# Score operands of 128 rows instead of 97, and the mixing of the experts as four pieces in separate steps

## The reference, cut to what matters

```python
sx = einsum('bsh,ndh->bnsd', x, hl_w) + hl_b          # 4 heads of 16 features
q  = einsum('bnsd,neod->bneso', sx, wq)               # 4 experts per head
k, v = ...                                            # one per head
scores = einsum('bnesd,bntd->bnest', q, k) * d**0.5 + causal
att = softmax(scores);  out = att @ v                 # per head and expert
gs  = softmax(out @ gate_w + gate_b)                  # weights of the experts
mixed = einsum('bnsed,bnse->bnsd', out, gs)           # the mixing of the experts
hn = layernorm(mixed + resid)
hx = layernorm(relu(hn @ fc1 + b1) @ fc2 + b2 + hn)
out = hx * softmax(hx @ fgate_w)                      # per head
```

## Time and profile before

| what | value |
|---|---|
| median of 3 runs | 1654.3 us (1645.82 to 1659.91) |
| the profiled execution | 1660.5 us, span 1658.4 us |
| mean granted TensorE clock | 0.84 |
| TensorE busy | 1356.7 us, 82% |
| VectorE, ScalarE, GpSimd busy | 53%, 47%, 25% |
| periods 0 to 7 (first exponential at 447.56 us, last one's end at 1590.79 us) | 1143.2 us |

### The profile page before, as it was taken

One profiled execution on the slowest core, in us unless ns is written; L12 is line 12 of the kernel. 1 busy time (PEld: TensorE's weight loads), 2 busy tenths in 40 slices (PEclk: granted clock), 3 DMA queues, 4 the chain that ended last, 5 costly groups with the idle time before them and its releaser, 6 DMA issues.

```text
span 1658.4 us, 28766 instructions
## 1 busy us (share of the span) xinstructions
PE 1356.7 (82%) x11103; PEld 641.5 (39%) x11103; DVE 881.7 (53%) x1824; ACT 774.5 (47%) x906; POOL 421.0 (25%) x619
## 2 busy tenths in 40 slices
PE   5888288924499889898988999998989889898942
PEld 3454287712154334333433424343343334333321
DVE  4667843375645534754474465447545644763343
ACT  0231144310166564466457446645754564576720
POOL 2000400053031231323314132322233241323421
PEclk9998699755599888789789878878997898899975
DMA  8995589022540280054018004600820370073000
GB/s 151 181 237 85 122 183 182 1 58 47 110 65 12 63 119 1 12 107 83 1 56 138 7 12 95 94 1 12 147 42 12 73 116 1 12 134 47 2 15 8
DMA packets 121399, 117.77 MB, mean 71 GB/s; under 512 B 73849, under 2 KB 90504, under 8 KB 121110
## 3 DMA queue, kind: packets, MB, share of 16 engines
q1 hardware_dynamic: 117216, 115.41, 37.3%
q10 hardware_dynamic: 3733, 0.60, 0.3%
q0 software_dynamic: 320, 0.04, 0.0%
HBM read 88.17 MB, written 22.95 MB: 67 GB/s over the span
## 4 chain that ended last, share of the span: by engine, by line
PE 44%; DVE 14%; DMA 5%; issue 4%; POOL 4%; ACT 3%; SPq 3%; POOLq 0%; DVEq 0%
PE b_pso L1959 14%; PE b_pss L1935 12%; PE b_psm L1986 4%; PE b_psm L2003 3%; ACT b_pb L2051 3%; POOL b_stat L2070 3%; DMA qk_parts_b<-b_qs 3%; PE b_psm L2015 2%; DMA b_qop<-bound_part 2%; PE b_psm L1998 2%; PE b_psm L1918 2%; PE b_psm L1995 2%; DVE b_rq L2191 1%; POOL b_pb L2089 1%; PE b_psm L2020 1%
## 5 line engine op out<-in xcount | busy, mean ns | idle before, releaser
L2051 ACT ACTIVATE b_pb<-b_pss 128x1024 f32<-128x1024 f32 (+2 forms) x736 | 666.9, 937 | 547.6 <-PE b_pss L1935 413.2
L2089 POOL TENSOR_SCALAR_AFFINE_SELECT b_pb<-b_pb 128x256 f32<-128x256 f32 (+1 forms) x544 | 232.1, 444 | 808.2 <-ACT b_pb L2051 803.2
L1959 PE MATMUL b_pso<-b_pb,b_vop 128*32 128x77 f32 (+4 forms) x5376 | 407.1, 416 | 31.9 <-POOL b_pb L2089 29.8
L1935 PE MATMUL b_pss<-b_qop,b_kop 97*128 97x512 bf16 (+3 forms) x1536 | 368.1, 357 | 28.9 <-issue 17.0
L1935 PEld LDWEIGHTS b_pss<-b_qop,b_kop 97*128 97x128 bf16 x1536 | 125.0, 106 | 260.5 <-ACT b_pb L2051 137.8
L1959 PEld LDWEIGHTS b_pso<-b_pb,b_vop 128*32 128x32 f32 x5376 | 123.0, 119 | 227.7 <-issue 175.3
L2272 DVE TENSOR_TENSOR b_ofm<-b_pso,b_mk 128x512 f32<-128x512 f32 (+1 forms) x96 | 51.8, 540 | 163.5 <-PE b_pso L1959 162.6
L2154 DVE COPY b_ot<-b_psm 128x336 f32<-128x336 f32 (+1 forms) x96 | 40.1, 418 | 149.2 <-PE b_psm L1986 148.9
L2070 POOL TENSOR_TENSOR b_stat<-b_stat,b_mh 128x18 f32<-128x18 f32 x34 | 109.1, 3226 | 38.8 <-DVE b_stat L2343 27.3
L1986 PEld LDWEIGHTS b_psm<-w_mixer,b_ofm 128*128 128x128 f32 (+1 forms) x576 | 81.0, 215 | 95.3 <-issue 58.7
L915 PE MATMUL psc<-tz,ub 128*64 128x128 f32 x1152 | 80.5, 285 | 44.2 <-DVE tz L1036 35.7
(11 more groups left out here) (378 smaller groups left out, 1542.0 us busy)
## 6 DMA issues: line engine op xcount, KB each, us to landing
b_qop<-qk_parts_b SPq DMA_DIRECT2D x192, 144.0 KB
tz<-taps SPq DMA_DIRECT2D x64, 304.0 KB, 9.6
x<-in_x SPq DMA_DIRECT2D x16, 1024.0 KB, 13.7
qk_parts_b<-b_qs SPq DMA_DIRECT2D x16, 864.0 KB, 5.2
b_kop<-qk_parts_b SPq DMA_DIRECT2D x192, 36.0 KB
b_mk<-b_mskf SPq DMA_DIRECT2D x128, 36.0 KB, 4.4
qk_parts_b<-b_ks SPq DMA_DIRECT2D x8, 432.0 KB, 3.9
n_late<-id_d SPq DMA_DIRECT2D x1, 2400.0 KB, 9.5
```

What stands on the lines that cost most here:

```text
L1935: mm = pe.matmul(pss[:, u % 2, b, col:col + w], lhs, qop[:, n, e, q0:q0 + w], start=True, stop=True, skip_group_check=True)
L1959: mm = pe.matmul(pso[VW * ee:VW * (ee + 1), (3 * n + x) % 2, q0 - QT * x:q0 - QT * x + w], vop[0:r, j, n, :], pb[0:r, slot_, b, cc:cc + w] ...
L2051: nc.scalar.activation(pb[:, s % PB, 0:nb, 0:w], pss[:, s % 2, 0:nb, 0:w], ACT.Exp, scale=float(HD) ** 0.5).then_inc(exped, 1)
L2089: ins = pool.affine_select(out=v_, in_=v_, compare_op=ALU.is_ge, fill=0.0, base=0, pattern=pat, channel_multiplier=-1)
```

## The change

Both operands of the scores get 128 partitions. GpSimd sets rows 96 to 127 of `qop` to zero as its second instruction of the stage, and those of `kop` behind its first root, before the row of -1. Row 96 of `qop` is then overwritten by SyncE's DMA, which waits for that memset; rows 97 to 127 of both stay zero. `late_ok` counts to 7 instead of 5. `head_mix` is cut into four parts: the gate (four small operations), the large product, the first addition, and the second addition with the residual. Group 0 has them at steps 63, 65, 67 and 69, group 1 at 8, 9, 10 and 11.

```diff
-        qop = sb("b_qop", [KB_, NH, NE, LP], BF16)
-        kop = sb("b_kop", [KB_, NH, LP], BF16)
+        qop = sb("b_qop", [P, NH, NE, LP], BF16)
+        kop = sb("b_kop", [P, NH, LP], BF16)
...
-        LOGITS, GEXP, MIX = (59, 5), (62, 8), (64, 9)
+        LOGITS, GEXP, MIX = (59, 5), (62, 8), ((63, 65, 67, 69), (8, 9, 10, 11))
...
                                 sp.wait_ge(bound_spilled, c * 16 + 16)
                                 sp.sem_inc(sp_passed, 1)
+                                if not att:
+                                    sp.wait_ge(late_ok, 1)
+                                    sp.sem_inc(sp_passed, 1)
...
-                                sp.wait_ge(late_ok, 5)
+                                sp.wait_ge(late_ok, 7)
...
-                        pe.wait_ge(late_ok, 5)
+                        pe.wait_ge(late_ok, 7)
...
                 pool.wait_ge(mh_ok, 1)
+                pool.memset(qop[KT:P].bitcast(F32), 0.0).then_inc(late_ok, 1)
+                pool.wait_ge(late_ok, 1)
...
                         pool.wait_ge(rstd, 1)
+                        pool.memset(kop[KT:P].bitcast(F32), 0.0).then_inc(late_ok, 1)
+                        pool.wait_ge(late_ok, 2)
                         pool.memset(kop[KT:KB_], -1.0).then_inc(late_ok, 1)
...
-                def head_mix(p, g):
-                    v.wait_ge(logit_exp, p * 2 + g + 1)
-                    ch.step(red(mxh[:], lg[:], AX.X, ALU.add))
...
+                def head_mix(p, g, part):
+                    if part == 0:
+                        v.wait_ge(logit_exp, p * 2 + g + 1)
+                        ch.step(red(mxh[:], lg[:], AX.X, ALU.add))
+                        ch.step(nc.vector.reciprocal(mxh[:], mxh[:]))
+                        ch.step(tt(lg[:], lg[:], bcast(mxh[:], NE), ALU.mult))
+                        ch.step(tt(lg[:], lg[:], rec[:], ALU.mult))
+                    elif part == 1:
+                        ch.step(tt(prod, pairof(g)..., bcast(lg[:], HD), ALU.mult))
+                    elif part == 2:
+                        ch.step(tt(half, prod[:, :, 0:2], prod[:, :, 2:4], ALU.add))
+                    else:
+                        ch.step(tt(quar, half[:, :, 0], half[:, :, 1], ALU.add))
+                        ch.step(tt(mixp(g), quar..., residp(g), ALU.add))
...
-                            if on_ and s == MIX[g]:
-                                head_mix(p - g, g)
+                            if on_ and s in MIX[g]:
+                                head_mix(p - g, g, MIX[g].index(s))
```

More of the change, by code:

```diff
@@ L2103, in run @@
                         pool.wait_ge(rstd, 1)
+                        pool.memset(kop[KT:P].bitcast(F32), 0.0).then_inc(late_ok, 1)
+                        pool.wait_ge(late_ok, 2)
                         pool.memset(kop[KT:KB_], -1.0).then_inc(late_ok, 1)
-                        pool.wait_ge(late_ok, 1)
+                        pool.wait_ge(late_ok, 3)
                         pool.memset(mk[:], 1.0).then_inc(late_ok, 1)
-                        pool.wait_ge(late_ok, 2)
+                        pool.wait_ge(late_ok, 4)
                         pool.memset(fxt[D:D + 1], 1.0).then_inc(late_ok, 1)
-                        pool.wait_ge(late_ok, 3)
+                        pool.wait_ge(late_ok, 5)
                         pool.memset(hx1[D:D + 1], 1.0).then_inc(late_ok, 1)
-                        pool.wait_ge(late_ok, 4)
+                        pool.wait_ge(late_ok, 6)
                         pool.memset(ot[:], 1.0).then_inc(late_ok, 1)
@@ L2240, in head_logits @@
                     tt(lg[:], lg[:], bcast(mxh[:], NE), ALU.subtract).then_inc(logit, 1)
-                def head_mix(p, g):
-                    v.wait_ge(logit_exp, p * 2 + g + 1)
-                    ch.step(red(mxh[:], lg[:], AX.X, ALU.add))
[L2246 to L2252, removed]
+                def head_mix(p, g, part):
[6 more added lines that the diff above has]
+                    elif part == 1:
+                        ch.step(tt(prod, pairof(g)[:, :, 0:D].rearrange("p g (e d) -> p g e d", d=HD), bcast(lg[:], HD), ALU.mult))
+                    elif part == 2:
+                        ch.step(tt(half, prod[:, :, 0:2], prod[:, :, 2:4], ALU.add))
+                    else:
+                        ch.step(tt(quar, half[:, :, 0], half[:, :, 1], ALU.add))
+                        ch.step(tt(mixp(g), quar.rearrange("p (n a) d -> p n a d", n=2), residp(g), ALU.add))
                 def put_values(n):
```

## The result

| | before | changed |
|---|---|---|
| median | 1655.86 us (4 runs, 1645.82 to 1659.91) | 1604.02 us (4 runs, 1593.76 to 1614.63) |
| profiled execution | 1660.5 us | 1604.14 us |
| mean granted clock, profiled | 0.840 | 0.878 |
| periods 0 to 7 | 1143.2 us | 1085.1 us (449.36 to 1534.46) |

The ratio of the times is 0.9696, with a 95% interval from 0.9619 to 0.9773: 3.0% faster. Periods 0 to 7 are 58 us shorter there, and start 1.8 us later.

A forecast was written before the change was run, and what follows sets the result against it. TensorE was taken to bound the kernel, partly waiting or at 1.2 GHz. Terms of 35 + 8.1 + 12.6 + 7.6 = 63 us, off the median of 1654.3, gave 1591 us; the forecast's own range was 1560 to 1612.

The forecast's parts named there:

- mixing of group 0: Steps 64 to 73: TensorE's wait for `ofm` goes and the clock stays up, 5.0 us per period, 35 us over seven.
- zero rows, steps 18 to 40: In periods 3 and 4 the two clock falls stay away, 4.0 us each, 8.1 us together.
- zero rows, steps 41 to 56: The clock rises earlier in four periods, 12.6 us, and one period of six has no drop, 7.6 us.
- both to stay away: The two clock falls, steps 18 to 26 and 27 to 40, expected gone: 2.73 + 1.31 = 4.0 us per period.
- two signs of the forecast: Signs of being right: steps 18 to 40 take 36.3 us in every period; mean clock rises from 0.84 to about 0.90.
- My reason for leaving the fall in: Steps 41 to 56: the drop comes in short, narrow matmuls (`tok`, L1995) that the change doesn't touch, so it was kept.
- The prices put at nothing: 128-row matmuls and weight loads (106 ns unchanged), `qop`'s memset (7.9 us, covered by idle time) and group 1's mixing cost nothing.
- rival 4: Slower: full 128-row weight loads in the scores take 112 ns more, 86 us in all, giving 1705 us; chance 0.04.
- sign of a missing cover: GpSimd: a root of period -1 starting after 383 us would show `qop`'s memset not covered, costing 7.9 us once.
- Rival 1: Zero rows do nothing for the clock, only the mixing helps: put at 1630 us; chance 0.16.
- rival 2: Only the rows help; in steps 64 to 73 VectorE bounds and the parts merely move the wait: 1626 us; chance 0.06.
- rival 3: Neither helps: the wait becomes one of step 68 and rows don't count, time within 1%; chance 0.04.

The follow-up runs named there:

- e1: The changed kernel with the scores' matmuls reading 97 rows again, memsets and mixing in pieces kept: 1621.63 us, ratio 0.9848 to the kernel before.
- e5: The changed kernel with the prologue's operands `xt` and `w_all` (65 rows) also padded with zeros to 128: 1564.26 us, ratio 0.9460 to the kernel before.
- e2: The changed kernel with 128 rows kept but the mixing again as one block at steps 64 and 9: 1617.17 us, ratio 0.9810 to the kernel before.
- e3: The changed kernel with ones instead of zeros in rows 97 to 127 of `qop`, those of `kop` still zero: 1598.69 us, ratio 0.9735.
- e7: The changed kernel with group 1 of the mixing as one block at step 9, group 0 in pieces: 1601.21 us, no ratio drawn.
- e8: The changed kernel with prologue and linear-layer operands also padded to 128 rows, but scores reading 97: 1575.21 us, ratio 0.9519 to the kernel before.
- e9: The changed kernel with prologue and linear-layer operands also padded to 128 rows, mixing as one block at steps 64 and 9: 1576.15 us, ratio 0.9523.

## Why the prediction was right, and where its sizes were off

The sign and the two causes held, and the size came out a little smaller: of the 63 us forecast, 55 are found in the stretches that the sum was made of, and 58 in periods 0 to 7 as a whole. Term by term, the kernel before against the changed one:

| term | forecast | measured |
|---|---|---|
| mixing of group 0 (steps 64 to 73) | 35 | 37.4 |
| zero rows, steps 18 to 40 | 8.1 | 3.1 |
| zero rows, steps 41 to 56 | 20.2 | 14.8 |
| not in the sum: steps 0 to 17 | 0 | 3.9 |
| not in the sum: steps 57 to 63 and 74 to 91 | 0 | -1.1 |

**The mixing.** The wait went (22.1 us to 0.3), L1989 moved up by 3.2 us, and VectorE became next. The path holds further on, too: in period 3 `qnorm` of step 70 starts on VectorE 13.5 us into the stretch (forecast 850.9 - 837.25 = 13.7), and the queries of step 72 on TensorE 14.1 us into it (forecast 14.7):

```profile
971.92 0.60 DVE L2187 TENSOR_SCALAR b_bound<-b_psm,b_kmax 16x384 f32<-16x384 f32 x1
```
```profile
972.57 0.91 PE L2006 MATMUL b_psm<-b_xt,w_all 65*128 65x384 f32 x2
```

Steps 64 to 73 take 16.4 us in five of periods 0 to 6 (17.0 and 18.2 in two) where 16.9 was the forecast. The extra comes from period 7, which I had left out: its low clock there went too (13.58 to 10.60 us). The clock stayed up by the pieces alone in all periods but one (e1); the rows weren't needed for it here. One thing was put at nothing and wasn't quite: TensorE's wait for the bound's row at the start of a period grew from 7.5 to 10.9 us over seven periods.

**Steps 18 to 40** was the step of the forecast that was over-sized: I had expected "both to stay away". The second fall did (24.0 to 24.2 us in each of periods 1 to 6). The first came back, shorter: steps 18 to 26 take 13.90 us at 0.88 in period 3 instead of 15.00 at 0.77. It went from period 1 and came in periods 5 and 7, which had none before; why in these, the runs don't show. In these steps TensorE waits for GpSimd, which makes roots before it gets to the masks of the probabilities. All waits for those masks sum up to 29.4 us, 29.2 before, and about half of that lies at step 24. The rows do nothing about them: e5, with the prologue at 128 rows as well, has this fall in seven periods. With the old rows (e1) the first fall is as short, 13.9 us, and the second comes in one of periods 1 to 6 (25.3 us). So the 3.1 us can't be put down to the rows, and what shortened these falls stays open. Period 1's fall, gone here, was not in the sum either. So two signs of the forecast failed: steps 18 to 40 take 37.9 us and not 36.3 in periods 3 to 5, and the mean clock rose to 0.878 and not to about 0.90.

**Steps 41 to 56.** The kind of outcome was right (one period of six without the fall, at 26.5 us, where 25.9 was estimated; the other kind 33.5). Period 6, at 33.55 us before, took 36.66, and period 1 took 35.1, where the forecast had put all at 33.5. That it was one period of six is luck: with the same rows e2 has one, e3 two and e7 none. Nor are all 14.8 us the rows': e1, with the old rows, has 6.4 of them, by where its falls came, which leaves 8.4. My reason for leaving the fall in, that its cause is the prologue's narrow matmuls, is what e5 shows: with these at 128 rows it is gone in every period. The scores' rows have a part in it still: with 97 of them beside a full prologue (e8) the clock falls in three of six.

**The prices put at nothing.** The weight load takes 103 ns with 128 rows and 103 with 97 (e1), and a pair of 512-column matmuls has 0.60 us in both kernels' timelines, so rival 4 has no ground. The memset of `qop` is covered by the idle time before the first root, as these rows of GpSimd's timeline in the changed kernel show:

```profile
373.29 7.77 POOL L2069 MEMSET b_qop<- 32x9216 f32 x1
384.54 1.81 POOL L2075 TENSOR_TENSOR b_statx<-b_statx,b_mh 128x9 f32<-128x9 f32 x1 [3.48 <-DVE b_statx L2233]
386.41 2.01 POOL L2109 MEMSET b_kop<- 32x2304 f32 x1
```

It took 7.77 us (7.9 forecast), and 3.48 us of idle time are left in front of the root. The forecast's sign of a missing cover, a root later than 383 us, came true and means nothing: the root stood at 383.14 before, and the whole stage starts 1.3 us later here. From the stage's first memset it is 11.44 us to the root, and was 11.33. Group 1's pieces cost and give nothing (e7).

**The rivals.** Rival 1 (zero rows do nothing) is refuted by e1 and e5, rival 2 (only the rows) by e1, rival 3 by both. Rival 2's path was taken in part: most of the wait's length did move on, to L2006 and L2013, but in shorter pieces, and the stretch got shorter all the same. The rule of the Trainium skill that was weighed ("TensorE: Matmul & The Clock Gate", Part 1: The HAM clock gate) has the clock follow how busy the engine has been, and names no rows. Here steps 41 to 56 are 32.97 of 33.52 us busy at a mean clock of 0.75 (e1) and 25.18 of 26.53 at 1.00 (e5), with the same matmuls but for the rows. The measurement decides against busy time as the whole of it.

## What to carry to other kernels

Where the granted clock is low although TensorE is busy, look at how many rows its matmuls name: padding operands of 65 or 97 rows with zeros to 128 cost no time per matmul here (0.91 us a pair in the prologue and 0.60 in the scores, either way) and gave back 1.1 to 1.5% for the scores and 2.4% more for the prologue. It does not help where the clock falls behind a wait that stays, as in steps 18 to 26. A wait of TensorE can cost more than its length: the 3.1 us here cost 5.5, because the clock fell behind it, and 2.0 where scores, prologue and linear layers had 128 rows (e9 against the pieces). So price a wait with its clock, and cut a long block of VectorE where the copy that TensorE waits for can go in between.

## What the runs showed of the hardware that was not expected

Rows of zeros in both operands hold TensorE's clock up (mean clock 0.866 without and 0.876 with them in the scores), and it makes no difference that the runs show whether one of the two operands has ones in them (0.8755). Whether rows with data in both would hold it better wasn't run. The effect of rows adds up over different kinds of matmuls: e8, with the prologue full and the scores narrow, has 0.8995, between 0.866 (scores narrow, prologue narrow) and 0.909 (both full); the changed kernel, with only the scores full, has 0.876. Whether single rows count or steps of several isn't settled: 112 rows gave 0.868.
